# Splitting sixteen experts' weights in two parts each, the last expert's ahead of the first block

## The reference, cut to what matters

```
scores = jax.nn.softmax(xt @ Wg.T, axis=-1)
...
topi = jax.lax.top_k(masked, TOPK)[1]
weights = jnp.take_along_axis(scores, topi, axis=1) * ROUTE_SCALE
combine = jnp.zeros((T, E), xt.dtype).at[jnp.arange(T)[:, None], topi].add(weights)
h = jax.nn.silu(jnp.einsum('td,eid->eti', xt, W1)) * jnp.einsum('td,eid->eti', xt, W3)
expert_out = jnp.einsum('eti,edi->etd', h, W2)
y = jnp.einsum('etd,te->td', expert_out, combine)
z = jax.nn.silu(xt @ Ws1.T) * (xt @ Ws3.T) @ Ws2.T
return (y + z).reshape(B, S, D)
```

## Time and profile before

| what | us |
|---|---|
| median of three runs | 792.77 |
| the three runs | 795.21, 792.46, 792.77 |
| the profiled execution: its own time | 795.21 |
| the profiled execution: span of the trace | 793.3 |
| PE busy in the span | 710.9 (90%) |
| DVE busy | 573.5 (72%) |
| ACT busy | 444.7 (56%) |
| POOL busy | 394.7 (50%) |
| mean granted clock of PE, as a share of full speed | 0.962 |

### The profile page before, as it was taken

How to read it: one execution, slowest core, us unless ns; L and a number is a source line. 1 busy time by engine, 2 the same in 40 slices (tenths; PEclk the granted TensorE clock), 3 DMA queues, 4 the chain that set the end, 5 groups by cost and what they waited for, 6 DMA issues and landing times. The chain is left out here.

```text
span 793.3 us, 12268 instructions
## 1 busy us (share of the span) xinstructions
PE 710.9 (90%) x3946; PEld 555.7 (70%) x3946; DVE 573.5 (72%) x1075; ACT 444.7 (56%) x969; POOL 394.7 (50%) x331
## 2 busy tenths in 40 slices
PE   8698877999999996999999999999889798999950
PEld 3244333598888885899998998898768456788840
DVE  6899999754353366888888888888889867344436
ACT  2897764353434335777776776776651467455430
POOL 0599878144675454544444223223322488577720
PEclk9699999999999999999999999999999999799985
DMA  5646511110344601120210124000068122233327
GB/s 143 281 147 245 192 65 42 61 40 22 110 130 131 202 21 48 41 74 27 74 60 21 34 69 176 1 1 1 21 220 320 50 82 81 74 97 100 98 81 230
DMA packets 38823, 77.66 MB, mean 98 GB/s; under 512 B 5345, under 2 KB 20394, under 8 KB 37738
## 3 DMA queue, kind: packets, MB, share of 16 engines
q1 hardware_dynamic: 34088, 64.41, 23.6%
q0 software_dynamic: 4512, 12.33, 5.2%
q10 hardware_dynamic: 162, 0.14, 0.1%
HBM read 59.07 MB, written 17.79 MB: 97 GB/s over the span
## 5 line engine op out<-in xcount | busy, mean ns | idle before, releaser
L1184 PE MATMUL psum<-xT_hi,w_ring 128*128 128x512 f32 x272 | 91.1, 395 | 1.0 <-ACTq L285 0.7
L2501 ACT ACTIVATE a_p_exp<-psum,a_nmax 128x256 f32<-128x256 f32 x128 | 59.5, 471 | 56.6 <-DVE a_nmax L2670 56.6
L2600 POOL TENSOR_TENSOR a_rr<-a_ss,eps 128x8 f32<-128x8 f32 x32 | 6.5, 205 | 157.0 <-DVE a_ss L2651 157.0
L641 POOL TENSOR_TENSOR m_dbu<-m_du,m_b_all 128x1024 f32<-128x1024 f32 x31 | 73.7, 2399 | 11.7 <-DVE m_du L727 9.1
L735 DVE TENSOR_TENSOR_SCAN m_hst<-psum,m_dbu 128x1024 f32<-128x1024 f32 x32 | 73.1, 2284 | 0.0
L1961 POOL DMA_INDIRECT expert_rows<-y_rows,f_puts_i x47 | 55.6, 1183 | 33.3 <-ACT y_rows L1907 32.4
L1320 POOL TENSOR_TENSOR f_h_lo<-f_hid,f_h_hi 128x512 fp32r<-128x512 f32 x34 | 44.0, 1293 | 44.8 <-ACT f_h_hi L1294 44.3
L387 PE MATMUL psum<-m_hc,ident 128*128 128x512 f32 x128 | 63.6, 620 | 0.0
L2364 PE MATMUL psum<-a_kT,a_qT 128*128 128x256 f32 x256 | 60.6, 379 | 1.4 <-ACT a_kT L2493 1.4
L1956 POOL DMA_INDIRECT x_rows<-norm_rows,f_rows_i x47 | 46.0, 979 | 28.8 <-DVE f_rows_i L2114 14.8
L1184 PEld LDWEIGHTS psum<-xT_hi,w_ring 128*128 128x128 f32 x272 | 51.1, 188 | 11.9 <-issue 1.5
(11 more groups left out here) (313 smaller groups left out, 2242.3 us busy)
## 6 DMA issues: line engine op xcount, KB each, us to landing
expert<-in_experts SPq DMA_DIRECT2D x16, 608.0 KB, 8.7
m_b_all<-b_rows SPq DMA_DIRECT2D x8, 1024.0 KB, 5.8
w_raw<-in_moe SPq DMA_DIRECT2D x20, 384.0 KB, 3.1
k_raw<-m_side SPq DMA_DIRECT2D x16, 256.0 KB, 2.0
a_keys<-k_raw SPq DMA_DIRECT2D x16, 256.0 KB, 2.6
norm_rows<-xn SPq DMA_DIRECT2D x8, 512.0 KB, 7.5
added<-expert_rows SPq DMA_DIRECT2D x16, 256.0 KB, 5.8
fold_in<-in_w_fold SPq DMA_DIRECT2D x8, 384.0 KB, 3.3
```

Source lines behind the costliest of these rows:

```text
L641: pool.tensor_tensor(dbu[:, k % DBU_RING, :, :], du[:, h, :, :], b_all[:, n:n + 1, :].to_broadcast([P, G, HALF]), ALU.mult).then_inc(dbu_r ...
L1184: mm = pe.matmul(dst, a[part], b[of], start=(k == 0 and i == 0), stop=(k == KD - 1 and i == 2), skip_group_check=True)
L2501: ins = act.activation(pe_[:, n % 2, m, :], bank(hh)[:, tile * L:(tile + 1) * L], ACT.Exp, bias=nmax[:, n % 2, m:m + 1], accum_out=rsum[:, ...
```

## The change

The 16 whole splits become 32 parts: of each expert first its 704 columns, then its 512. `parts` lists them in the order 15, 12, 13, 14, 0, 1, ..., 11. Both parts of expert 15 stand ahead of the loop (`SPLIT_AHEAD = 1`); on ACT between the last `gated` and the last `hidden_hi` of the shared expert, on DVE behind the pad. Behind blocks 0 to 11 stand two parts each, behind blocks 5 and 8 three (`WIDE_SPLITS`), behind blocks 12 to 15 one each. `places()` moves behind block 1's parts and `weights_found()` behind block 3's.

```
+SPLIT_AHEAD = 1
+WIDE_SPLITS = (5, 8)
...
-        def split_at(n):
-
-            return n + FP32_BLOCKS if n < experts - FP32_BLOCKS else n - (experts - FP32_BLOCKS)
+        early = list(range(experts - 1, experts - 1 - SPLIT_AHEAD, -1))
+        parts = [(e, part) for e in early + [e for e in range(FP32_BLOCKS, experts) if e not in early] + list(range(FP32_BLOCKS))
+                 for part in range(2)]
+
+        def split_cols(n):
+
+            return parts[n][0], (slice(0, KD * FW), slice(KD * FW, EXP_W))[parts[n][1]]
+
+        def splits_behind(i):
+
+            if i < 0:
+                return range(0, 2 * SPLIT_AHEAD)
+            first = 2 * SPLIT_AHEAD + sum(halves_of(j) for j in range(i))
+            return range(first, first + halves_of(i))
+
+        def halves_of(i):
+
+            if i < FP32_BLOCKS:
+                return 3 if i in WIDE_SPLITS else 2
+            return 1 if i < experts else 0
...
         def splits_before(i):
 
-            return i - FP32_BLOCKS + 1 if i < experts else experts
+            return max(n for n, (e, _) in enumerate(parts) if i >= experts or FP32_BLOCKS <= e <= i) + 1
...
+                def expert_high(n):
+                    e, cols = split_cols(n)
+                    act.activation(experts_hi[:, expert_at(e, cols.start, cols.stop - cols.start)], experts_w[e][:, cols], ACT.Copy)\
+                        .then_inc(split_hi, 1)
+
                 for j in range(J0 + 1, J1):
                     gated(j)
+                    if j == J1 - 1:
+                        act.wait_ge(w.up_ps, J1)
+                        act.wait_ge(sparse.experts_in, 16 * experts)
+                        for n_ in splits_behind(-1):
+                            expert_high(n_)
                     hidden_hi(j)
+                act.wait_ge(w.down_s, J1)
...
-                    if i < experts:
-                        expert_high(i)
+                    for n_ in splits_behind(i):
+                        expert_high(n_)
...
-                places()
-                weights_found()
+
+                def expert_low(n):
+                    e, cols = split_cols(n)
+                    if e < FP32_BLOCKS:
+                        dve.wait_ge(y_ps, e + 1)
+                    dve.wait_ge(split_hi, n + 1)
+                    at = expert_at(e, cols.start, cols.stop - cols.start)
+                    dve.tensor_tensor(experts_lo[:, at], experts_w[e][:, cols], experts_hi[:, at], ALU.subtract).then_inc(split, 1)
+
+                for n_ in splits_behind(-1):
+                    expert_low(n_)
...
-                    if i < experts:
-                        expert_low(i)
+                    for n_ in splits_behind(i):
+                        expert_low(n_)
+                    if i == 1:
+                        places()
+                    if i == 3:
+                        weights_found()
```

More of the change, by code:

```diff
@@ L1643, in whole_products @@
             return i < FP32_BLOCKS
-        def split_at(n):
-            return n + FP32_BLOCKS if n < experts - FP32_BLOCKS else n - (experts - FP32_BLOCKS)
+        early = list(range(experts - 1, experts - 1 - SPLIT_AHEAD, -1))
[12 more added lines that the diff above has]
+            return 1 if i < experts else 0
+        assert 2 * SPLIT_AHEAD + sum(halves_of(i) for i in range(NB)) == 2 * experts
         def expert_at(e, at, width):
@@ L1907, in block_out @@
                     act.activation(y_rows[:, i % PUTS, :], y_bank(i)[:, 0:DM], ACT.Copy).then_inc(y_s, 1)
[L1909 to L1914, removed]
                 rows_kept(0)
@@ L2184, in rows_low @@
                     dve.tensor_tensor(xT_lo[:, i % XR, :], xT_bank(i)[:, 0:DM], xT_hi[:, i % XR, :], ALU.subtract).then_inc(xT_lo_s, 1)
[L2186 to L2193, removed]
                 for i in range(NB + 1):
```

## The result

The changed kernel takes 789.67 us (median of 11 executions, 787.28 to 794.93) against 792.84 for the kernel before (11 executions, 791.71 to 797.88). The ratio is 0.9946, with a 95% interval of 0.9922 to 0.9970: 0.54% faster, about at the bound of what this kernel's measurement can tell. The forecast was 789.8, with a range of 787.2 to 793.2.

What follows compares the result with a forecast made beforehand. PE was taken as the bound, held by a ring of three engines and by a clock fall behind block 16. Order 1.5 and clock 3.94 made 5.4 us off the profiled 795.21: 789.8, range 787.2 to 793.2.

Steps and rivals of the forecast that it cites:

- The clock term: Behind block 16: the fall follows the 1.36 us wait, which shrinks to 0.75; if it stays away, 3.94 us return.
- The order: 0.6 us gained ahead of the loop, 1.3 lost in blocks 0 to 11, 2.2 gained in blocks 12 to 16: 1.5.
- The gain in blocks 12 to 16: Stalls of 3.15 us fall to 0.95, with 0.2 left at block 12 and 0.75 at the last wait: gain 2.2.
- The sum: 1.5 us from order and 3.94 from the clock make 5.4 off the profiled execution's 795.21: 789.8.
- The price of a part: 704 columns: 0.89 us on DVE, 0.79 on ACT; two parts back to back occupy DVE 1.42 instead of 1.35.
- The ring: Blocks 0 to 11: transposes to down product 3.48 us instead of 3.83, PE ready at 3.43; ordinary stalls at most 0.05.
- rival 3: Parts pay their full fixed cost on DVE, 1.58 us for two, eating the order's gain: 791.3; chance 0.07.
- A sign of being wrong: Ordinary down products over 3.1 us apart, PE awaiting gathered rows, DVE part over 0.9, or new stretch at 0.50.
- POOL at nothing: Gather, scatter, gaps and blocking in the loop make 2.9 us, under PE's 3.04 a block, so no effect.
- Rival 1: Clock falls all the same behind block 16 or a little elsewhere; only the order's 1.5 remains: 791.2 to 793.7; chance 0.23.
- Rival 2: Stalls at blocks 0 and 1, 1.55 us together, bring the fall there: 794.8, or 798.7 with block 16's; chance 0.07.
- Rival 4: Routing steps and third parts fall into unseen slack; half of 3.7 us of stalls gone: 788; chance 0.13.

Runs made afterwards that it cites:

- long last wait: Changed kernel with no third part behind blocks 5 and 8 and three parts instead of one behind block 15; 793.25 us, ratio 0.9995 to the kernel before.
- halves alone: Against the changed kernel: two parts behind each of blocks 0 to 15, old expert order, none ahead, routing steps ahead of the loop; 789.71 us, ratio 0.9950.
- small part first: Changed kernel with the 512 columns of each expert ahead of its 704; 790.81 us, ratio 0.9957 to the kernel before.
- routing ahead: Changed kernel with places() and weights_found() back ahead of the loop, behind the last expert's two parts; 791.47 us, ratio 0.9972.
- in gaps: Changed kernel with three parts ahead, a third part behind block 8 only, routing steps behind blocks 0, 1 and 20; 786.09 and 786.98 us.
- four ahead: Against the run with routing in gaps: four parts ahead, no third part, smaller part first in fp32 blocks; 786.27 us, ratio 0.9891 to the kernel before.
- one expert ahead alone: Changed kernel with whole splits: one expert ahead of the loop, one behind each of blocks 0 to 14, none behind 15; 790.60 us, ratio 0.9962.
- the third profile: The kernel before, unchanged, profiled a third time in a single execution; 794.03 us.

## Why the prediction came out, point by point

The last three columns are of each profile; "three blocks" is from block 16's first product to block 19's.

| kernel | wait ahead of block 16 | clock behind it | three blocks |
|---|---|---|---|
| before, three profiles | 1.36, 1.47, 1.72 | 0.50 each time | 11.89, 11.92, 9.40 |
| long last wait | 2.00 | 0.50 | 11.97 |
| halves alone | 1.44 | 0.50, short | 9.36 |
| small part first | 0.96 | 1.00 | 7.96 |
| changed, two profiles | 0.46, 0.57 | 1.00 | 7.96, 7.82 |
| routing ahead; in gaps (two); four ahead | 0.51; 0.43, 0.44; 0.63 | 1.00 | 7.85; 7.97, 7.97; 7.80 |
| one expert ahead alone | none | 1.00 | 8.32 |

**The clock term: its mechanism was right, its size differs from execution to execution.** In five of five profiles with a wait of 1.36 or more at this place the clock fell, in eight of eight with 0.96 or less it did not, and putting the wait back brought the fall back. In the pair of profiles that the sum used, 11.89 - 7.96 = 3.93 us came back, as forecast. But 3.94 is the price of a ten-us fall: of the five falls two lasted some 3.4 us and cost 1.4 to 1.5. For the median the prediction supposed such shorter falls, and put the 2.4 us by which its profiled execution lay above the median down to them. That shorter falls occur is shown; that they make up the 2.4 is not.

The step "with no such stretch left, they should come to the same 789.8" failed for the profiled execution. It took 792.48, because it was 2.82 late at block 0, by its start and by falls ahead of the loop; the second profile of the changed kernel took 787.97. Over all executions the mean granted clock is 0.9649 in 23 of the changed kernel and 0.9620 in 91 of the kernel before. (1 - clock) x 2 x span gives 55.4 and 60.2 us at half speed, 4.8 less. At 3.94 / 10 = 0.39 per us that is some 1.9 us. This is an estimate: it takes the price behind block 16 for every stretch, and the scatter of the executions allows for 0.7 to 3.1.

**The order: 2.0 measured, 2.3 between the second profiles, 1.5 forecast.** Ahead of the loop PE's wait for `b_hid` fell from 1.29 to 0.79 and 0.68, forecast 0.6 less. Blocks 0, 1, 3, 5 and 8 stall for 0.51, 0.90, 0.77, 1.05 and 0.34, forecast 0.6, 0.95, 0.6, 0.85 and 0.6; with blocks 7 and 10 4.0 in all, forecast 3.7. The gain in blocks 12 to 16 was under-rated: they take 11.38 instead of 11.7, since blocks 13 and 14 come every 2.56 us, not 2.65, and PE does not wait at block 12, where 0.2 had been left. Block 15 takes 3.42 from its first product to block 16's; the chain of copy, part and PE had been worked out as 3.40. The wait in it is 0.46 and 0.57, not 0.75: PE was ready 2.96 and 2.87 behind block 15's first product, not 2.65.

**The sum.** Order 2.0 to 2.3 and clock 1.9 are 3.9 to 4.2, where the medians differ by 3.2 and 3.6, which the scatter of the clock's estimate covers. The forecast had 1.5 + 3.94 against a profiled execution 2.4 above the median, that is 3.0 below the median. Its order is 0.5 to 0.8 too small, its clock term some 2.0 too large over all executions, and the 2.4, whose source no run shows, makes up for that. So it is in part luck that the median came within 0.2 of 789.8. In the profiled pair the loop gave what was forecast and more, 2.0 + 3.9, and 2.8 was lost ahead of it.

**The price of a part was right.** The line of the changed kernel for all parts (shortest, median and longest in ns):

```profile
L2192 DVE TENSOR_TENSOR experts_lo<-expert,experts_hi x32: 681/814/894, 627.3 to 676.8; 128x704 fp32r<-128x704 f32 x16, 128x512 fp32r<-128x512 f32 x16
```

0.69 and 0.89 us, as estimated, and two back to back run 1.49 from start to end, against 1.43 of a whole. The page of the Trainium skill that the prediction set against the split (VectorE: DVE Perf Modes, the TRN2 errata) has the fixed price of each instruction exposed; it asks for 512 elements or more, which both parts have. By the full durations the two would take 0.69 + 0.89 = 1.58. The rows show 0.06 more than a whole, so most of the fixed price is hidden, and rival 3 falls.

**The ring: right on average, wrong in its detail.** From the transposes of gathered rows to the down product it takes 3.47 us (647.35 to 650.82 in the run with the long last wait), forecast 3.48. But PE is not always ready 3.43 behind its transposes: there it was ready 3.22 behind, so every second block stalled by 0.25, not "at most 0.05", and a pair took 6.18 us. A sign of being wrong came true with it: down products of ordinary blocks more than 3.1 us apart, 647.57 to 650.82. In the gap version a pair took 6.10, with halves alone 6.11 and later 6.18, both with no listed stall. What sets the one pattern or the other stays open; the order of the parts does not.

**POOL at nothing: right.** PE waits for no gathered rows in the loop. The scatters within blocks 0 to 16 even got shorter. The line of POOL's scatters from 626 to 678, before and then after (busy us, mean ns):

```profile
L1961 POOL DMA_INDIRECT expert_rows<-y_rows,f_puts_i x15 | 24.1, 1606 | 8.6 <-ACT y_rows L1907 7.7 <-issue 0.9
```

```profile
L1986 POOL DMA_INDIRECT expert_rows<-y_rows,f_puts_i x15 | 17.5, 1169 | 13.6 <-ACT y_rows L1939 12.9 <-issue 0.6
```

By the Trainium skill (SBUF — State Buffer, who interferes with whom) a DVE instruction with two SBUF inputs contends with a GpSimd instruction that reads SBUF. The rows agree that a scatter beside such an instruction is longer than the 0.99 of one alone, and show by how much: by what is left of the DVE instruction that runs when it starts. Before, 640.13 + 1.43 - 640.58 = 0.98 was left, and the scatter took 0.98 + 0.87. After, with a part that ends at 641.30, it was 0.53, and the scatter took 0.53 + 0.87:

```profile
639.81 1.49 DVE L2192 TENSOR_TENSOR experts_lo<-expert,experts_hi 128x704 fp32r<-128x704 f32 x2 [0.69 <-ACT experts_hi L1903]
640.77 1.40 POOL L1986 DMA_INDIRECT expert_rows<-y_rows,f_puts_i  x1 [0.96 <-ACT y_rows L1939]
```

That is why the scatters got shorter; that the cause is this port, no run isolates.

**The rivals.** Rival 1 did not happen at block 16. New stretches at 0.50, a sign of being wrong, did come ahead of the loop in both profiles of the changed kernel, but as the third profile shows they come in the kernel before as well. Rival 2 did not happen in the changed kernel, whose stalls at blocks 0 and 1 stay at 0.90 or less; its mechanism is real, as the profile with the routing ahead shows behind 2.71 us, at a price of some 1.1 us. Rival 4 did not happen either, but more than its gain of 1.8 lay open: put into gaps, the same work gave 48.8 us instead of 51.0.

## What to carry to other kernels

Where a long step stands in a ring of two engines, cut it in two so that the second engine starts on the first half: here that alone gained 0.36 us of 6.5 a pair of blocks, though the two parts cost 0.06 more. A ring without slack charges an inserted step in full (the third part behind block 5, 0.81 us, raised the stall there to 1.05 from the 0.25 of the run without it), so put side work where the engine is seen to wait, and keep the last wait ahead of a long dense stretch short. Take the price of a clock fall from several executions, not from the one that was profiled, and compare two profiles from the same step on, since they can differ by microseconds before it.

## What the runs showed of the hardware

At block 16 a wait of PE of 1.36 to 2.00 us was followed by a granted clock of 0.50 for some 3.4 or some ten us in each of five profiles, although PE was busy all through it; a wait of 0.96 us or less was not, in any of eight. Elsewhere the length of the wait does not decide: waits of 1.35 to 1.64 us ahead of block 0 were followed by none, in the profiles of the kernel before and of the halves alone, and one of 2.71 us there was followed by one. In the windows 305 to 312 and 617 to 624 the clock was 1.00 in one profile of the kernel before and 0.76 and 0.53 in another, so a fall at one place and its length are a matter of the execution as well. Why was not tested.

The same transfer at the start of the program took 7.4 us from issue to landing in one profile of the changed kernel and 5.1 in the other. And an indirect DMA of POOL that starts while a DVE instruction with two SBUF inputs runs took the rest of that instruction and 0.87 us more, where one alone takes 0.99.
